# Shared experts cut into 384 and 320 rows, with one merged chunk, in a cross-attention and expert kernel

## The reference, cut to what matters

```python
def _shared_swiglu(x, wg, wu, wd):
    return jax.nn.silu(x @ wg.T) * (x @ wu.T) @ wd.T
...
g = jnp.einsum('ecd,efd->ecf', buf, w_gate)
u = jnp.einsum('ecd,efd->ecf', buf, w_up)
eo = jnp.einsum('ecf,edf->ecd', jax.nn.silu(g) * u, w_down)
...
return y + _shared_swiglu(hidden_states, sh_gate, sh_up, sh_down)
```

## Time and profile before

| | |
|---|---|
| median of 3 runs | 1804.43 us |
| the profiled execution's own time | 1801.53 us |
| its span, first to last instruction | 1799.8 us |
| mean granted clock of TensorE | 0.975 of 2.4 GHz |
| PE busy | 1729.6 us (96%) |
| DVE, ACT, POOL busy | 1092.2, 1028.9, 743.2 us |
| chain of waits, by line | L2392 36%, L2410 19% |

### The profile page before, as it was taken

The page is one execution under the profiler, slowest core; times in us unless marked ns, Lnnn a source line. Parts: engine busy times, 40 slices in busy tenths (PEclk is TensorE's granted clock), DMA queues, the critical chain, the costliest instruction groups (busy, mean ns, idle before and its releaser), DMA issues.

```text
span 1799.8 us, 36496 instructions
## 1 busy us (share of the span) xinstructions
PE 1729.6 (96%) x12110; PEld 1583.7 (88%) x12110; DVE 1092.2 (61%) x2166; ACT 1028.9 (57%) x1879; POOL 743.2 (41%) x711
## 2 busy tenths in 40 slices
PE   4799999999999989999999999999999999999997
PEld 3588888888888889999999999999999999999986
DVE  6555556777667553433666666666666666666645
ACT  3567766666545452222566666666666666666645
POOL 6513222334223220142155555554554555555533
PEclk8989999999899999999999999999999999999978
DMA  5533433333322422312477777767777777777765
GB/s 179 151 112 100 117 106 95 118 97 94 98 71 78 164 99 91 119 37 72 153 223 210 237 211 212 235 206 214 229 211 217 222 212 222 227 204 229 224 176 171
DMA packets 149083, 289.89 MB, mean 161 GB/s; under 512 B 29198, under 2 KB 66318, under 8 KB 139648
## 3 DMA queue, kind: packets, MB, share of 16 engines
q1 hardware_dynamic: 116112, 238.21, 40.5%
q0 software_dynamic: 32880, 50.51, 13.4%
HBM read 243.73 MB, written 64.52 MB: 171 GB/s over the span
## 4 chain that ended last, share of the span: by engine, by line
PE 86%; DVE 4%; issue 4%; ACT 3%; POOL 1%; DVEq 1%; DMA 1%; SPq 0%; ACTq 0%; POOLq 0%
PE ps L2392 36%; PE ps L2410 19%; PE ps L1446 7%; PE ps L1454 5%; PE ps L1427 4%; PE ps L2375 3%; PE ps L1417 3%; PE ps L1443 2%; PE ps L1469 1%; PE ps L2714 1%; PE ps L1402 1%; PE ps L1463 1%; DVE nmax L645 1%; DVEq L647 1%; ACT gu_hi L2611 0%
## 5 line engine op out<-in xcount | busy, mean ns | idle before, releaser
L2142 POOL DMA_INDIRECT out<-y,ids_s x128 | 204.7, 1599 | 281.4 <-ACT y L2273 256.5
L2392 PE MATMUL ps<-xt_hi,gu_hi 128*128 128x256 f32 (+1 forms) x1920 | 313.9, 285 | 0.0
L2392 PE MATMUL ps<-xt_lo,gu_hi 128*128 128x256 f32 (+1 forms) x1920 | 299.9, 278 | 0.0
L2392 PE MATMUL ps<-xt_hi,gu_lo 128*128 128x256 f32 (+1 forms) x1920 | 299.2, 278 | 0.0
L2177 DVE TENSOR_TENSOR gu_lo<-raw_gu,gu_hi 128x1408 fp32r<-128x1408 f32 x132 | 214.5, 1625 | 113.9 <-ACT gu_hi L2174 107.8
L2392 PEld LDWEIGHTS ps<-xt_hi,gu_hi 128*128 128x128 f32 (+1 forms) x1920 | 259.6, 180 | 6.9
L1106 ACT ACTIVATE prob<-ps 128x512 f32<-128x512 f32 x256 | 152.1, 596 | 197.4 <-PE ps L1427 175.6
L2392 PEld LDWEIGHTS ps<-xt_lo,gu_hi 128*128 128x128 f32 (+1 forms) x1920 | 252.2, 179 | 0.0
L2392 PEld LDWEIGHTS ps<-xt_hi,gu_lo 128*128 128x128 f32 (+1 forms) x1920 | 251.8, 179 | 0.0
L2122 POOL DMA_INDIRECT xg<-h_rows,ids_g x128 | 192.5, 1504 | 119.7 <-POOL ids_g L2117 50.6
L2230 ACT ACTIVATE h_hi<-h 128x256 fp32r<-128x256 f32 (+1 forms) x240 | 100.4, 418 | 226.1 <-DVE h L2299 225.6
(11 more groups left out here) (305 smaller groups left out, 3032.1 us busy)
## 6 DMA issues: line engine op xcount, KB each, us to landing
raw_gu<-in_w_gu SPq DMA_DIRECT2D x71, 1408.0 KB, 8.0
raw_d<-in_w_d SPq DMA_DIRECT2D x71, 512.0 KB
raw_d<-in_w_d SPq DMA_DIRECT2D x71, 192.0 KB
qs<-qk_rows SPq DMA_DIRECT2D x192, 64.0 KB
ks<-qk_rows SPq DMA_DIRECT2D x192, 64.0 KB
xa<-in_x SPq DMA_DIRECT2D x16, 256.0 KB, 3.0
qk_rows<-k_hi SPq DMA_DIRECT2D x16, 256.0 KB, 2.2
qk_rows<-k_lo SPq DMA_DIRECT2D x16, 256.0 KB, 2.5
```

The source lines that it names most:

```text
L2142: pool.indirect_dma_start(out=out, out_offset=bass.IndirectOffsetOnAxis(B.ids_s[:, p, k:k + 1], 0), in_=B.y[:, p, k, :], in_offset=None, b ...
L2392: last = pe.matmul(gu_banks(c, m)[half], w[:, p, half, d, o:o + m], x[:, x_p, d, 0:W], start=i == 0, stop=i == len(steps) - 1)
```

## The change

The shared expert's 704 hidden rows are cut into 384 and 320 instead of twice 352. An even shared item has three chunks of 128. An odd one has two of 128 and a rest of 64 rows, whose 64 up columns and 64 gate columns stand next to each other as one stationary operand of 128 columns: 12 matmuls write up into PSUM partitions 0 to 63 and gate into 64 to 127. For the down product of the rest, ACT writes the high part of h a second time into partitions 64 to 127, and the high part of the down weights into partitions 64 to 127 of `d_lo`, so that one matmul with 128 rows does high by low and high by high together. The host lays out the shared weights to fit. Apart from that, PE reads `many` before `down` of the last item, and no longer waits for `y_taken` behind it. The routed items and the work in a third are as before.

```diff
+SH_COLS = (3 * P, FS - 3 * P)
+SH_REST = P // 2
...
+def gu_span(it, half):
+
+    if it.shared:
+        n = DC * SH_COLS[it.half]
+        begin = it.half * 2 * DC * SH_COLS[0] + half * n
+    else:
+        n = DC * F
+        begin = (it.half * 2 + half) * n
+    return begin, begin + n
...
+def merged(it, c):
+
+    return it.shared and it.half == 1 and c == NF - 1
+
+
+def rows_of_chunk(it, c):
+    if it.shared:
+        return SH_REST if merged(it, c) else P
+    return FCH[c][1]
...
-    def gu_banks(c, m):
-
-        bank = ps[0:m, GU0 + c % sets]
-        return bank[:, 0:W], bank[:, W:2 * W]
+    def gu_banks(it, c):
+
+        bank, m = ps[:, GU0 + c % sets], rows_of_chunk(it, c)
+        if merged(it, c):
+            return bank[m:2 * m, 0:W], bank[0:m, 0:W]
+        return bank[0:m, 0:W], bank[0:m, W:2 * W]
...
+    def merged_columns(tensor, it, d):
+
+        begin = gu_span(it, 0)[0] + 2 * DC * 2 * P + d * 2 * SH_REST
+        return flat_gu(tensor)[:, begin:begin + 2 * SH_REST]
...
             eng.activation(B.d_hi[:, p, 0:2], B.raw_d[:, p, 0:2], ACT.Copy)
-            eng.activation(B.d_hi[0:96, p, 2], B.raw_d[0:96, p, 2], ACT.Copy).then_inc(d_hi.sem, 1)
+            if merged(it, 2):
+                eng.activation(B.d_lo[m:2 * m, p, 2], B.raw_d[0:m, p, 2], ACT.Copy)
+            eng.activation(B.d_hi[0:m, p, 2], B.raw_d[0:m, p, 2], ACT.Copy).then_inc(d_hi.sem, 1)
...
         def high(it, c):
-            m = FCH[c][1]
+            m = rows_of_chunk(it, c)
             act.wait_ge(h_ready.sem, h_ready.value(it.e, c + 1))
             if c == 0 and (it - 2).exists:
                 down_done(act, it - 2)
+            if merged(it, c):
+                act.activation(B.h_hi[m:2 * m, it.half, c, 0:W], B.h[0:m, (it.half * NF + c) % 2, 0:W], ACT.Copy)
             act.activation(B.h_hi[0:m, it.half, c, 0:W], B.h[0:m, (it.half * NF + c) % 2, 0:W], ACT.Copy).then_inc(h_hi.sem, 1)
...
+            steps = [(w, x, d) for w, x in ((B.gu_hi, B.xt_hi), (B.gu_hi, B.xt_lo), (B.gu_lo, B.xt_hi))
+                     for d in range(DC)]
+            if merged(it, c):
                 for i, (w, x, d) in enumerate(steps):
-                    last = pe.matmul(gu_banks(c, m)[half], w[:, p, half, d, o:o + m], x[:, x_p, d, 0:W],
+                    last = pe.matmul(ps[:, GU0 + c % sets, 0:W], merged_columns(w, it, d), x[:, x_p, d, 0:W],
                                      start=i == 0, stop=i == len(steps) - 1)
+            else:
+                for half in range(2):
+                    for i, (w, x, d) in enumerate(steps):
+                        last = pe.matmul(gu_banks(it, c)[half], gu_columns(w, it, half, d, c), x[:, x_p, d, 0:W],
+                                         start=i == 0, stop=i == len(steps) - 1)
             last.then_inc(gu_ready.sem, 1)
...
                 steps = [(h, w, c) for h, w in ((B.h_hi, B.d_hi), (B.h_hi, B.d_lo), (B.h_lo, B.d_hi))
-                         for c in range(NF)]
+                         for c in range(NF) if not (merged(it, c) and h is B.h_hi and w is B.d_hi)]
                 for i, (h, w, c) in enumerate(steps):
-                    m = FCH[c][1]
+                    m = 2 * SH_REST if merged(it, c) and h is B.h_hi else rows_of_chunk(it, c)
...
             thirds["gate_up"](pe, FIRST, 0)
+            many.append(thirds["how_many"](pe))
             down(it)
             pe.wait_ge(h_ready.sem, h_ready.value(it.e, NF))
-            pe.wait_ge(y_taken.sem, y_taken.value(it.rows, nb))
 
         drive(pe, slot, after, side)
+        return many[0]
...
+    def how_many(eng):
+        eng.wait_ge(A["over_made"], 1)
+        return eng.value_load(over[0:1, E:E + 1], min_val=0, max_val=E)
+
+    def each(eng, body, many=None):
 
         LONG = N * TOPK // (2 * P + 1)
         GROUP = 8
-        eng.wait_ge(A["over_made"], 1)
-        many = eng.value_load(over[0:1, E:E + 1], min_val=0, max_val=E)
+        many = how_many(eng) if many is None else many
...
+        cols = lambda w: w.reshape(-1, DC, P).transpose(2, 1, 0).reshape(P, -1)
+        a, b = SH_COLS[0], FS - SH_REST
+        return c(np.concatenate([cols(gate[0:a]), cols(up[0:a]), cols(gate[a:b]), cols(up[a:b]),
+                                 cols(np.concatenate([up[b:], gate[b:]]))], 1))
```

More of the change, by code:

```diff
@@ L2002, in gu_rows @@
         if it.shared:
-            return ins["sh_gu"][it.half]
+            return ins["sh_gu"][:, gu_span(it, 0)[0]:gu_span(it, 1)[1]]
         return ins["w_gu"][bass.ds(it.expert, 1)].rearrange("a p n -> p (a n)")
@@ L2007, in d_rows @@
         if it.shared:
-            return ins["sh_d"][it.half]
+            return ins["sh_d"][it.half * SH_COLS[0]:it.half * SH_COLS[0] + SH_COLS[it.half], :]
         return ins["w_d"][bass.ds(it.expert, 1)].rearrange("a f n -> (a f) n")
@@ L2027, in slots_of, with gu_columns @@
         return routed[:, bass.ds(it.expert * CB, nb)]
-    def gu_banks(c, m):
-        bank = ps[0:m, GU0 + c % sets]
-        return bank[:, 0:W], bank[:, W:2 * W]
+    def gu_banks(it, c):
[3 more added lines that the diff above has]
+        return bank[0:m, 0:W], bank[0:m, W:2 * W]
+    def gu_columns(tensor, it, half, d, c):
+        o, m = c * P, rows_of_chunk(it, c)
+        if not it.shared:
+            return tensor[:, it.half, half, d, o:o + m]
+        begin = gu_span(it, half)[0]
+        if it.half == 0:
+            begin += d * SH_COLS[0] + o
+        else:
+            wide = 2 * P
+            begin = gu_span(it, 0)[0] + half * DC * wide + d * wide + o
+        return flat_gu(tensor)[:, begin:begin + m]
+    def merged_columns(tensor, it, d):
+        begin = gu_span(it, 0)[0] + 2 * DC * 2 * P + d * 2 * SH_REST
+        return flat_gu(tensor)[:, begin:begin + 2 * SH_REST]
     def chunk(item, c, back):
@@ L2168, in cut_gu @@
         p = it.half
-        hi, raw = B.gu_hi[:, p, half], B.raw_gu[:, p, half].rearrange("p (c f) -> p c f", c=DC)
+        begin, end = gu_span(it, half)
+        hi, lo = flat_gu(B.gu_hi)[:, begin:end], flat_gu(B.gu_lo)[:, begin:end]
+        raw = B.raw_gu[:].rearrange("p q a n -> p (q a n)")[:, begin:end]
         if act:
@@ L2176, in cut_gu @@
             eng.wait_ge(gu_hi.sem, gu_hi.value(it.weights, half + 1))
[L2177 removed]
+            eng.tensor_tensor(lo, raw, hi.bitcast(F32), ALU.subtract).then_inc(gu_lo.sem, 1)
     def cut_d(eng, it, act):
@@ L2181, in cut_d @@
             return
-        p = it.half
+        p, m = it.half, rows_of_chunk(it, 2)
         if act:
@@ L2222, in silu @@
                 act.wait_ge(h_ready.sem, h_ready.value(j.e, n + 1))
-            act.activation(B.sg[0:m, (it.half * NF + c) % 2, 0:W], gu_banks(c, m)[0], ACT.Silu).then_inc(sg_ready.sem, 1)
+            act.activation(B.sg[0:m, (it.half * NF + c) % 2, 0:W], gu_banks(it, c)[0], ACT.Silu).then_inc(sg_ready.sem, 1)
         def high(it, c):
-            m = FCH[c][1]
+            m = rows_of_chunk(it, c)
             act.wait_ge(h_ready.sem, h_ready.value(it.e, c + 1))
@@ L2378, in tensor_program @@
     def tensor_program(pe, thirds, side):
+        many = []
         def gate_up(it, c):
-            o, m = FCH[c]
-            p, x_p = it.half, it.rows_parity
+            x_p = it.rows_parity
             if c == 0:
@@ L2777, in _ @@
                 side = A["tensor"](pe, net)
-                items["tensor"](pe, thirds, side)
-                thirds["tensor"](pe)
+                many = items["tensor"](pe, thirds, side)
+                thirds["tensor"](pe, many)
 def program(nc, ins, out):
```

33 lines of the change are left out of this document (17 added, 16 removed).

## The result

| | before | changed |
|---|---|---|
| median of 22 runs each | 1804.39 us | 1794.01 us |
| lowest | 1792.87 us | 1786.58 us |
| ratio of the fast runs | | 0.9952, interval 0.9933 to 0.9971 |
| profiled execution, its span | 1801.53, 1799.8 us | 1793.65, 1791.9 us |
| mean granted clock | 0.975 | 0.977 |

The interval is one of 95%. The ratios leave out the few executions that took over 1.5% more than the fastest of the same kernel, among them the kernel before at 2551.78 us. The ratio is 8.7 us (0.0048 x 1804.4), where 13.7 were forecast (1801.5 - 1787.8); the medians differ by 10.4, and the spans of the two traces by 7.9 us. To see where they come from I cut every trace at three instructions: A is the start of the first matmul that reads `h2T` in slot 0, B the start of `down` of item 16, C the second `y` of item 79, and D the end of the span.

What follows compares the result with a forecast made beforehand. PE was taken to bound the shared items, with a mixed chain of waits at the end. Gate/up and down -14.6, slot 0's wait -0.2, the end +1.1: 1801.5 - 14.6 - 0.2 + 1.1 = 1787.8 us, predicted 1788, range 1782 to 1798.

Steps and rivals of the forecast that it cites:

- Gate/up, 10.9 us: Odd shared items: each of 8 loses 12 gate/up matmuls at 0.114 us, 10.9 us saved.
- rival G: Merged chunk of the odd shared items runs at half pace, 10.9 us lost again, 1798.7 us; 2%.
- Down, 3.7 us: Odd shared items: each loses 2 down matmuls at 0.233 us, 16 in all, 3.7 us saved.
- Wide weights, copies, slot table, 0: Shared items: 128-column loads, second copies of h_hi and down weights, and the slot table's 2.6 us reserve cost 0.
- E: A wait opens in the shared items and takes 5 us, with a dip of the clock, 1793 us; 7%.
- F: Wide weight loads of the even shared items reach the path, 5.2 us less gained, 1793 us; 3%.
- The end, +1.1: Behind the last item: 2.43 us gap goes, PE idles 8.4 us a third later, clock falls; second y 1.1 us later.
- A: At the end the clock stays up through the 8.4 us of idle PE, 1783.9 us; 10%.
- B: At the end the clock falls, one down does not restore it, one further third is slow, 1795.8 us; 17%.
- C: At the end POOL doesn't hold; the whole gap and slow stretch are regained, 1776.3 us; 7%.
- D: Clock remains at 1.2 GHz to the end of the thirds, slower than before, 1803.8 us; 4%.
- my own case: Whole kernel: the main forecast of 1788 us, reaching from 1785 to 1792 by itself; kept 50%.

Runs made afterwards that it cites:

- e1: Changed kernel with the 64-row step of each odd shared item's down filled up to 128 rows, h_lo with zeros; 0.9891 of the kernel before.
- e3: Changed kernel with the 64-row step of both passes of an odd shared item's down left out; 0.9910 of the kernel before.
- e4: Changed kernel with the side-by-side down passes undone: nine steps a pass, three on 64 rows, in odd shared items; 1.0031 of the kernel before.
- e2: Changed kernel with the two 64-row steps of an odd shared item's down placed one behind the other; 0.9917 of the kernel before.
- e5: Changed kernel with the edit at the end undone, so PE waits for y of the last item again; 0.9946 of the kernel before.
- e6: Kernel before with the edit at the end alone, shared experts as before; 0.9993 of the kernel before.
- e7: Changed kernel with POOL's copy of the slot weights moved ahead of its wait for the last scatter; 0.9916 of the kernel before.
- e9: As e8, but POOL copies only the weights early, and two thirds ahead; 0.9842 of the kernel before.
- e8: Changed kernel with e1 and e7 together, and the third down step on 128 rows in routed items and thirds too; 0.9836 of the kernel before.

## Why the prediction was right in the whole and wrong in a term

- **Gate/up, 10.9 us: right.** The merged chunk took 1.38 us for its 12 matmuls, the pace forecast. The 24 matmuls in its place took 2.82, so each item gave 1.44 us, 11.5 in all, and rival G is out.
- **Down, 3.7 us: the term that was mis-sized.** I multiplied 16 removed matmuls by 0.233, as if those that remained kept their pace. The edit also turned 96-row steps into steps on 64 rows, two in each odd `down`, and each of those stalls PE (e1 and e3 show it). The odd `down` went from 4.20 to 4.34 us: the term is -0.14 x 8 = -1.1 instead of +3.7. The even `down`, now on 128 rows throughout, gave 0.11 each and lost 0.09 in the chunk behind it (834.24 to 837.08 is 2.84 us for 24, 2.75 in the earlier trace rows). The chunks behind an odd `down` lost 0.09 too (5.56 for 5.47). So 8 x (1.44 - 0.14 + 0.11 - 0.09 - 0.09) = 9.8 us for the stage, and 9.9 were measured. Of the 4.8 us that this sum lacks against the 14.6 forecast, `down` itself stands for 4.0 and the chunks behind it for 1.4; gate/up gave 0.6 back. No row of the kernel before has a 64-row matmul in the items; a bound for it was missing from the sum altogether.
- **Wide weights, copies, slot table, 0: right.** No wait of PE stands in slots 1 to 16. Rivals E and F did not happen: the 48 matmuls with the widened chunk took 5.54 us from start to start (837.43 to 842.97), in the kernel before 5.54 to 5.69. Slot 0's wait fell from 4.14 to 3.91 us.
- **The end, +1.1: right mechanism, too small in this trace.** It measured +2.3. POOL waited 10.79 us for the landing where 9.53 was taken over from before, so `y` of the first third came 19.7 us behind that of item 79 instead of 18.7; from there to the second `y` it took 15.2 us, and 15.0 were forecast. The landing is what varies: in the five kernels with this same end POOL waited 9.29, 10.34, 10.41, 10.74 and 10.79 us (e3, e4, e1, e2, changed), and C to D took 65.89, 66.69, 67.00, 67.26 and 67.70, which is 0.5 to 2.3 over before. The dip of the clock at 1732, not forecast either, cost nothing. The row of e3:

```profile
1736.55 0.19 POOL L2649 COPY wsl<-w 128x1 f32 x1 [9.29 <-issue]
```

  e5, e6 and e7 show the cause. Rivals A to D are out: the clock fell, came back within one `down`, the thirds behind followed at 11.0 and 10.9 us, and POOL did hold.

With the two misses (4.7 and 1.2 us) the forecast of 1788 becomes 1793.9, and 1794.0 was measured. That lies beyond the 1785 to 1792 of my own case. It lies in the range only because that reached to 1798 for the sake of B, a slow third that did not happen: that the range held is luck, though the ways in which each term works, the stall aside, were as forecast.

What stays open: why the gate/up matmuls right behind a `down` got slower in the shared slots. They take 0.118 us each behind an even `down` of the changed kernel and behind both in e1, 0.116 behind an odd `down` of the changed kernel, and 0.114 in the kernel before. The `down` ahead is not the reason by itself: in slot 16 of the changed kernel, a routed item, the same 24 matmuls take 2.74 us (0.114 each) behind a `down` that runs on 128 rows throughout:

```profile
858.78 0.63 PE L2454 MATMUL ps<-xt_hi,gu_hi 128*128 128x256 f32 x4
...
861.52 0.60 PE L2431 MATMUL ps<-ident,xg 128*128 128x128 f32 x4
```

Open too are the last thirds of e7 and e9 (13.4 and 12.5 us), where PE was idle 1.3 and 1.5 us behind `xt_lo` and the clock was low after it. In the third ahead of each, PE had waited 0.7 and 0.8 us for gathered rows, which POOL had asked for late, but I did not try an earlier gather.

## What to carry to other kernels

Before matmuls are counted out, look at the shapes of those that stay: one on 64 rows among full ones cost as much as two and a half, and the same step filled up with zeros to 128 rows cost 0.35 less. A wait taken away in front of a bottleneck is worth only what the next one leaves; find who holds that (here a 0.2 us copy queued behind a landing) and move it first, then the same edit pays 7 us. And cut traces at fixed instructions: the shared and routed stages repeat within 0.5 us, while the attention ahead of them spreads by 14.

## What was not expected of the hardware

- A weight load of 64 rows is not hidden behind a matmul on 128 rows, nor the next load of 128 rows behind it: 0.35 and 0.24 us idle on the loader.
- A `down` step on 96 rows costs 0.02 us more than on 128: 18 steps take 4.20 against 4.09 us, six of them on 96 rows. Timelines of PE, in a routed item of the changed kernel and in one of e8:

```profile
962.26 0.86 PE L2472 MATMUL ps<-d_hi,h_hi 128*128 128x512 f32 x3
...
966.47 0.52 PE L2454 MATMUL ps<-xt_hi,gu_hi 128*128 128x256 f32 x3
```

```profile
965.97 0.86 PE L2479 MATMUL ps<-d_hi,h_hi 128*128 128x512 f32 x3
...
970.06 0.63 PE L2461 MATMUL ps<-xt_hi,gu_hi 128*128 128x256 f32 x4
```
